# Two cross-attentions on one core: seven of eight context transposes move from TensorE to VectorE, fed by a second, permuted load

## The chip, the cores and the metric

One core of a Trainium2 chip runs the whole program. The metric is device time in microseconds (us). Single instructions are given in ns.

## The reference

```python
# 8 batches; x is 8 x 100 x 128, ctx is 8 x 1444 x 128; 16 heads of width 64
normed = x * rsqrt(mean(x * x) + eps) * norm_w
q, k, v = heads(normed @ wq), heads(ctx @ wk), heads(ctx @ wv)
x = x + (softmax(q @ k.T) @ v) @ wo          # first cross-attention
x = x + softmax(x @ ctx.T) @ ctx             # second one, ctx is key and value
```

## The kernel before

The weights are folded: with Wq·Wk of a head multiplied out beforehand, the keys of all heads are the context itself, and with Wv·Wo multiplied out the values are too. So one batch is 1,600 rows of queries (16 heads x 100), cut into 13 items of up to 124 rows, each against the same 1,444 tokens. The second attention of a batch is one more item of 100 rows ("late" in the code); for batches 0 to 5 it runs in step 8 of the batch after. For precision each operand is split in a high and a low part in fp32r, and three products are summed.

A batch has 14 steps, 0 to 13, written out by hand for each engine. In step s an item is scored, and the item of the step before is turned. "Item 9" below means the item scored in step 9. For it:

- TensorE makes the scores in three chunks of 512, 512 and 420 tokens (`scores`, lines 912, 913, 916), in a ring of four PSUM banks.
- VectorE takes the maximum of each chunk (`chunk_maximum`, L697), and then of the three (L702).
- ScalarE takes the exponentials (`exp_chunk`, L555).
- In the next step TensorE turns the probabilities (`turn`, L940), chunk by chunk, into `ps_t`, which has two banks. A turn waits until the low part of the chunk two turns earlier has been read from its bank (`wait_turn_bank`). The list `TURNS` holds the order.
- ScalarE copies the turned chunk as the high part (`turned_chunk_hi`, L546), and VectorE makes the low part (`turned_chunk_lo`, L683).
- TensorE multiplies turned probabilities with the context (`pv`, L964), 17 matmuls in steps 10 and 11, none in step 12, where the late item's product stands after the turns (`pv_late`, L977 to L981).

The scores need the context with its features on the partitions (`cT_hi`, `cT_lo`). In steps 9, 10 and 11 of batches 0 to 6, TensorE ends its step with four transposes of the next batch's context (`turn_ctx`, L874 and L876; one chunk per step) into the same two banks. ScalarE copies this as `cT_hi` after the second exponential of the step (L612). VectorE makes `cT_lo` (L683) behind the low parts of its step. The order of VectorE in a step is:

```python
chunk_maximum(g, 0)
turned_chunk_lo(prev, 0)
chunk_maximum(g, 1)
chunk_maximum(g, 2)          # and the maximum of the three, L702
turned_chunk_lo(prev, 1)
turned_chunk_lo(prev, 2)
# cT_lo in steps 9, 10, 11; invert; pair_lo
```

Odd batches 1, 3 and 5 make the queries of two later batches in steps 5 to 10, 12 and 13: a pair of heads a step, with a copy on ScalarE (`pair_hi`, L500) ahead of `cT_hi` and one on VectorE (`pair_lo`) behind `cT_lo`. Batch 0 makes the Wv·Wo products in steps 9 to 12 instead (L1033).

The queue of SP loads the context of the next batch in step 2 (`load_ctx`, L322 and three small ones, L324). For each group of items it stores the inverted denominators to DRAM (L361), waits for that, and loads them back broadcast over the partitions (L368). GpSimd multiplies with them (`norm_group`, L437): group 1 in step 7, ahead of its own work on the item of that step (`split_tail`, L429 and L431), which TensorE's third turn of the next step waits for.

Of the kernel before, what the change touches and what calls it, by code (L numbers as in the profile page):

```python
# [16 lines left out]
def bass_two_cross_attentions(nc, x, ctx_in, wq, wk, wv, wo, norm_w, out):  # L17
# [26 lines left out]

    def rows(item):
        return Q if item == LATE else min(TM, R - TM * item)
# [32 lines left out]
    CTX_T_STEPS = [9, 10, 11]  # L79
    CTX_SPLIT = [(0, 4), (4, 8), (8, 12)]  # L80
# [34 lines left out]
    for g, (b, s, _, _) in enumerate(ITEMS):  # L115
        if g > 0 and g < L_FIRST:
            TURNS += [("item", g - 1, c) for c in range(NC)]
        if b < B - 1 and s in CTX_T_STEPS:
            TURNS.append(("ctx", b + 1, CTX_T_STEPS.index(s)))
# [6 lines left out]
    def ev(g, c=NC - 1):  # L126
        return NC * g + c + 1
# [30 lines left out]
    with ExitStack() as stack:  # L158
# [18 lines left out]
        c_both = [sb(f"c_both{i}", [P, SLOTS, 2, D], F32R) for i in range(2)]  # L177
        cT_hi = [sb(f"cT_hi{i}", [P, S], F32R) for i in range(2)]
        cT_lo = [sb(f"cT_lo{i}", [P, S], F32R) for i in range(2)]
        tail_a = sb("tail_a", [P, D])  # L180
# [27 lines left out]
        pT_late = sb("pT_late", [P, SLOTS, 2, Q], F32R)  # L208
# [3 lines left out]
        pT = [sb(f"pT{i}", [P, SLOTS, 2, GW[i]], F32R) for i in range(2)]  # L212
# [73 lines left out]
        ctx_turned = sem("ctx_turned")  # L286
        ctxT_hi = sem("ctxT_hi")
# [31 lines left out]
        def _(sp):  # L319
# [7 lines left out]

            def store_result(b):
                sp.wait_ge(fin_ready, b + 1)
                sp.dma_start(out[b:b + 1, :, :].rearrange("a q d -> (a q) d"), result[0:Q, :])\  # L330
                    .then_inc(stored, 16)
# [13 lines left out]
            for b in range(B):  # L345
                if b < B - 1:
                    sp.wait_ge(ctx_turned, n(b, NC, NC - 1))
                    sp.wait_ge(ctx_lo_done, n(b, len(CTX_SPLIT), len(CTX_SPLIT) - 1))
                    sp.wait_ge(stack_steps, n(b, 3, 2))
                    load_ctx(b + 1)  # L350
                for g in range(NG):
                    if g == NG - 1 and 0 < b < B - 1:
                        store_result(b - 1)
                    if b == B - 1 and g == NG - 1:
                        continue
                    k = NG * b + g
                    t0, count = GROUPS[g][0], len(GROUPS[g])
                    s0 = step_of(t0)
                    cols = slice(TM * t0, TM * (t0 + count))
                    sp.wait_ge(inverted, k + 1)  # L360
                    sp.dma_start(scratch[b:b + 1, cols].rearrange("a (t p) -> p (a t)", p=TM),  # L361
                                 rinv[0:TM, s0:s0 + count],
                                 allow_slow_non_contiguous=True).then_inc(rinv_stored, 16)
                    sp.wait_ge(rinv_stored, 16 * (k + 1))
                    if k >= 2:

                        sp.wait_ge(o_normed, k - 1)
                    sp.dma_start(rinv_row[:, k % 2, 0:TM * count],  # L368
                                 scratch[b:b + 1, cols].to_broadcast([P, TM * count]))\
                        .then_inc(rinv_row_loaded[g], 16)  # L370
# [5 lines left out]
        def _(pool):  # L376
# [9 lines left out]
            pool.memset(ones[:, :], 1.0).then_inc(consts_begun, 1)  # L386
            pool.wait_ge(consts_begun, 6)
# [11 lines left out]
            def split_ctx(b, part):  # L399
                lo, hi = CTX_SPLIT[part]  # L400
                top = min(hi, FULL)
                pool.wait_ge(ctx_hi_done, n(b, len(CTX_SPLIT), part))
                pool.tensor_tensor(c_both[b % 2][:, lo:top, 1, :], ctx_raw[:, lo:top, :],
                                   c_both[b % 2][:, lo:top, 0, :].bitcast(F32),
                                   ALU.subtract).then_inc(ctx_lo_done, 1)

            def stack_tail(b):
# [10 lines left out]
                pool.tensor_tensor(c_both[b % 2][:, FULL, 0, :], tail_a[:, :], tail_b[:, :], ALU.add)\  # L418
# [64 lines left out]
        def _(act):  # L483
# [41 lines left out]
            def ctx_hi(b, part):  # L525
                lo, hi = CTX_SPLIT[part]
                top = min(hi, FULL)
                act.activation(c_both[b % 2][:, lo:top, 0, :], ctx_raw[:, lo:top, :], ACT.Copy)\
                    .then_inc(ctx_hi_done, 1)

            def turned_chunk_hi(g, c):
# [4 lines left out]
                if item == LATE:  # L536
                    if c == 0 and bb > 0:
                        act.wait_ge(pv_done, block(bb - 1, LATE))
                    dst = pT_late[:, j0:j0 + nj, 0, 0:m]
                else:  # L540
                    grp, col = group_of(item), group_col(item)
                    if c == 0 and NG * bb + grp >= 2:
                        b2, g2 = divmod(NG * bb + grp - 2, NG)
                        act.wait_ge(pv_done, block(b2, g2))
                    dst = pT[grp % 2][:, j0:j0 + nj, 0, col:col + m]
# [29 lines left out]
            for b in range(B):  # L575
                for s in range(STEPS):
# [24 lines left out]
                    if here:  # L601
                        for c in range(NC):
# [3 lines left out]
                            if c == 1 and s in CTX_T_STEPS and b < B - 1:  # L606
                                ct = CTX_T_STEPS.index(s)
                                c0, w = CHUNKS[ct]
                                act.wait_ge(ctx_turned, n(b + 1, NC, ct))
                                if ct == 0 and 0 < b < B - 1:  # L610
                                    act.wait_ge(scored, ev(late_number(b - 1)))
                                act.activation(cT_hi[(b + 1) % 2][:, c0:c0 + w],  # L612
                                               ps_t[:, turn_bank("ctx", b + 1, ct), 0:w], ACT.Copy)\
# [40 lines left out]
        def _(dve):  # L654
# [50 lines left out]
            def turned_chunk_lo(g, c):  # L705
# [5 lines left out]
                if item == LATE:  # L711
                    dst, hi = [pT_late[:, j0:j0 + nj, a, 0:m] for a in (1, 0)]
                else:
                    grp, col = group_of(item), group_col(item)
                    dst, hi = [pT[grp % 2][:, j0:j0 + nj, a, col:col + m] for a in (1, 0)]
# [44 lines left out]
            for b in range(B):  # L760
                for s in range(STEPS):
# [15 lines left out]
                    if s in CTX_T_STEPS and b < B - 1:  # L777
# [3 lines left out]
                        lo_part(cT_lo[(b + 1) % 2][:, c0:c0 + w], ps_t[:, turn_bank("ctx", b + 1, ct), 0:w],  # L781
                                cT_hi[(b + 1) % 2][:, c0:c0 + w], ctxT_lo)
                    if prev is not None:
# [44 lines left out]
        def _(pe):  # L828
# [89 lines left out]
            def wait_turn_bank(what, at, c):  # L918
                k = TURNS.index((what, at, c)) - 2
                if k >= 0:  # L920
                    what, at, c = TURNS[k]
                    if what == "ctx":
                        pe.wait_ge(ctxT_lo, n(at, NC, c))
                    else:
                        pe.wait_ge(turned_lo, ev(at, c))
# [18 lines left out]
            def pv(b, grp, lo, hi, by_chunk=False):  # L944
# [13 lines left out]
                for i in range(lo, hi):  # L958
# [3 lines left out]
                    weights = c2[:, j, (0, 0, 1)[part], :]  # L962
                    moving = p[:, j, (0, 1, 0)[part], 0:w]
# [4 lines left out]
            def pv_late(bb, by_chunk=False):  # L968
# [5 lines left out]
                for j in range(FULL):  # L974
                    if by_chunk and j % 4 == 0:
                        pe.wait_ge(turned_lo, ev(g, j // 4))
                    pe.matmul(ps_o[0:Q, 0, 0:2 * D], pT_late[:, j, 0, :],  # L977
                              c2[:, j, :, :].rearrange("p a d -> p (a d)"), start=(j == 0), stop=False)
                    pe.matmul(ps_o[0:Q, 0, 0:D], pT_late[:, j, 1, :], c2[:, j, 0, :],  # L979
                              start=False, stop=False)  # L980
                pe.matmul(ps_o[0:Q, 0, 0:D], pT_late[:, FULL, 0, :], c2[:, FULL, 0, :],  # L981
# [81 lines left out]
            for b in range(B):  # L1063
                for s in range(STEPS):
# [21 lines left out]
                    if s in CTX_T_STEPS and b < B - 1:  # L1086
                        c = CTX_T_STEPS.index(s)
                        if c == 0:
                            pe.wait_ge(ctx_loaded, 64 * (b + 2))
                        wait_turn_bank("ctx", b + 1, c)  # L1090
                        turn_ctx(ps_t[:, turn_bank("ctx", b + 1, c)], c).then_inc(ctx_turned, 1)
# [64 lines left out]
```

## Time and profile before

| | |
|---|---|
| time, median of 3 runs | 699.72 us (698.96 to 700.08) |
| the profiled execution's own time | 699.38 us |
| its span in the profile | 697.6 us |
| TensorE matmul busy | 675.7 us, 97% of the span |
| VectorE busy | 465.6 us, 67% |
| ScalarE busy | 467.8 us, 67% |
| GpSimd busy | 160.7 us, 23% |
| mean granted clock of TensorE | 0.995 |
| DMA packets | 25,566 |

PE is the matmul side of TensorE, DVE is VectorE, ACT is ScalarE, POOL is GpSimd, SPq is the queue of SP. A busy share says how much of the span an engine had an instruction under way. It does not say how late the next one can come.

### The profile page before, as it was taken

The page shows a single profiled execution, that of the slowest core. Times are in us where ns is not written, and L with a number is a line of the kernel's source. Part 1 is how long each engine was busy: PE and PEld are TensorE (multiplying, and loading weights), DVE is VectorE, ACT ScalarE, POOL GpSimd, SP SyncE. Part 2 cuts the span into 40 slices and gives each one's busy share as a digit, 9 for nine tenths or more (in the row PEclk, how much of TensorE's full clock was granted, in tenths as well). Part 3 has the DMA queues.
Part 4 walks back from the last instruction along what each step waited for, and adds up shares of the span by engine and source line. Part 5 has one row for each costly group of instructions (what it writes and reads, how often), then busy time and mean ns, then how long its engine had stood idle before and what let it go on. Part 6 is the DMA issues. An engine that isn't in the chain of part 4 may idle for free. (4 is left out here: it accounts for less than half of the span.)

```text
span 697.6 us, 13322 instructions
## 1 busy us (share of the span) xinstructions
PE 675.7 (97%) x4764; PEld 613.6 (88%) x4764; DVE 465.6 (67%) x994; ACT 467.8 (67%) x1169; POOL 160.7 (23%) x485
## 2 busy tenths in 40 slices
PE   5899999999999999999999999999999999999986
PEld 4688989998999889999899889999899888999885
DVE  3586666777567875677666775677766776577733
ACT  4767676677666766667766776667766777666742
POOL 2211133111322114111142114211142212422110
PEclk9999999999999999999999999999999999999997
DMA  6012112111021002220121111202013011112000
GB/s 188 1 54 16 8 12 53 16 8 9 15 55 15 16 1 23 53 16 8 16 51 11 16 9 15 55 14 16 1 15 60 9 16 15 9 9 16 9 12 7
DMA packets 25566, 16.50 MB, mean 24 GB/s; under 512 B 14334, under 2 KB 23838, under 8 KB 25502
## 3 DMA queue, kind: packets, MB, share of 16 engines
q1 hardware_dynamic: 25502, 15.66, 14.7%
q8 instruction: 39, 0.64, 0.5%
q14 instruction: 25, 0.20, 0.2%
HBM read 15.19 MB, written 0.46 MB: 22 GB/s over the span
## 5 line engine op out<-in xcount | busy, mean ns | idle before, releaser
L546 ACT ACTIVATE pT<-ps_t 128x496 fp32r<-128x496 f32 (+1 forms) x312 | 182.4, 587 | 179.8 <-PE ps_t L940 177.6
L697 DVE TENSOR_REDUCE part_max<-ps_s 124x1 f32<-124x512 f32 (+2 forms) x336 | 209.5, 651 | 60.1 <-PE ps_s L916 59.0
L964 PE MATMUL ps_o<-pT,c_both 128*128 128x248 f32 (+2 forms) x1632 | 242.9, 291 | 0.6 <-DVE result L748 0.5
L683 DVE TENSOR_TENSOR pT<-ps_t,pT 128x496 fp32r<-128x496 f32 (+3 forms) x312 | 192.0, 623 | 69.5 <-ACT pT L546 67.7
L964 PEld LDWEIGHTS ps_o<-pT,c_both 128*128 128x128 f32 x1632 | 219.4, 189 | 3.6 <-DVE pT L683 2.6
L555 ACT ACTIVATE probs<-ps_s,neg_max 124x512 f32<-124x512 f32 (+2 forms) x336 | 219.1, 663 | 1.4 <-DVE neg_max L702 1.4
L940 PE MATMUL ps_t<-ident,probs 124*128 124x124 f32 (+2 forms) x1232 | 184.1, 268 | 5.1 <-DVE pT L683 1.9
L940 PEld LDWEIGHTS ps_t<-ident,probs 124*128 124x128 f32 (+2 forms) x1232 | 146.1, 140 | 44.8 <-ACT probs L555 10.1
L429 POOL CAST tails<-probs 124x36 fp32r<-124x36 f32 (+2 forms) x224 | 40.6, 213 | 489.7 <-ACT probs L555 489.7
L912 PE MATMUL ps_s<-cT_hi,q_hi 128*124 128x512 f32 (+3 forms) x312 | 143.5, 460 | 1.2 <-DVE q_lo L683 1.2
L916 PE MATMUL ps_s<-cT_hi,q_lo 128*124 128x512 f32 (+3 forms) x312 | 118.8, 381 | 0.0
L913 PE MATMUL ps_s<-cT_lo,q_hi 128*124 128x512 f32 (+3 forms) x312 | 118.6, 380 | 0.0
L555 ACT ACTIVATION_READ_ACCUMULATOR probs<-ps_s,neg_max 124x1 f32 (+2 forms) x336 | 70.2, 209 | 0.0
L916 PEld LDWEIGHTS ps_s<-cT_hi,q_lo 128*124 128x124 f32 (+1 forms) x312 | 57.2, 183 | 10.8
L912 PEld LDWEIGHTS ps_s<-cT_hi,q_hi 128*124 128x124 f32 (+1 forms) x312 | 57.9, 186 | 2.1 <-issue 0.8
L913 PEld LDWEIGHTS ps_s<-cT_lo,q_hi 128*124 128x124 f32 (+1 forms) x312 | 58.3, 187 | 0.1
L683 DVE TENSOR_TENSOR cT_lo<-ps_t,cT_hi 128x512 fp32r<-128x512 f32 (+1 forms) x23 | 15.2, 662 | 34.3 <-ACT cT_hi L612 29.2
L683 DVE TENSOR_TENSOR q_lo<-ps_m,q_hi 128x400 fp32r<-128x400 f32 x31 | 17.7, 572 | 30.5 <-ACT q_hi L500 30.5
L437 POOL TENSOR_TENSOR o_norm<-o_norm,rinv_row 128x248 f32<-128x248 f32 (+2 forms) x47 | 35.8, 761 | 3.4 <-ACT o_norm L562 3.3
L986 PE MATMUL ps_m<-o_norm,wvo 128*128 128x100 f32 x256 | 33.0, 272 | 1.6 <-DVE o_norm L740 1.6
L986 PEld LDWEIGHTS ps_m<-o_norm,wvo 128*128 128x128 f32 x256 | 31.4, 191 | 1.8 <-DVE o_norm L740 1.8
L431 POOL TENSOR_TENSOR tails<-probs,tails 124x36 fp32r<-124x36 f32 (+2 forms) x112 | 29.3, 261 | 9.0
(130 smaller groups left out, 492.8 us busy)
## 6 DMA issues: line engine op xcount, KB each, us to landing
ctx_raw<-in_ctx_dram SPq DMA_DIRECT2D x8, 704.0 KB
rinv_row<-denominator_rows SPq DMA_DIRECT2D x39, 124.0 KB, 3.7
rinv_row<-denominator_rows SPq DMA_DIRECT2D x8, 186.0 KB, 3.5
denominator_rows<-rinv SPq DMA_DIRECT2D x39, 1.0 KB
wq_sb<-in_L_xattn_wq_dram SPq DMA_DIRECT2D x2, 256.0 KB, 6.1
wk_sb<-in_L_xattn_wk_dram SPq DMA_DIRECT2D x2, 256.0 KB, 6.3
wv_sb<-in_L_xattn_wv_dram SPq DMA_DIRECT2D x1, 512.0 KB, 7.8
wo_sb<-in_L_xattn_wo_dram SPq DMA_DIRECT2D x1, 512.0 KB, 8.9
```

What stands on the lines that cost most here:

```text
L429: pool.tensor_copy(t[0:m, c * TAIL:(c + 1) * TAIL].bitcast(F32R), src).then_inc(tail_hi, 1)
L437: pool.tensor_tensor(o_norm[:, group_cols(g)], o_norm[:, group_cols(g)], rinv_row[:, (NG * b + g) % 2, 0:group_width(g)], ALU.mult).then_i ...
L546: act.activation(dst, ps_t[:, turn_bank("item", g, c), 0:nj * m] .rearrange("p (j m) -> p j m", m=m), ACT.Copy).then_inc(turned_hi, 1)
L555: act.activation(probs[g % 2][0:m, c0:c0 + w], ps_s[0:m, score_bank(g, c), 0:w], ACT.Exp, bias=neg_max[0:m, k:k + 1], accum_out=sums[0:m, ...
L683: dve.tensor_tensor(dst, src, hi.bitcast(F32), ALU.subtract).then_inc(done, 1)
L697: mx = dve.tensor_reduce(part_max[0:m, k, c:c + 1], ps_s[0:m, score_bank(g, c), 0:CHUNKS[c][1]], AX.X, ALU.max)
L912: pe.matmul(dst, a_hi, cT_hi[bb % 2][:, c0:c0 + w], start=True, stop=False)
L913: pe.matmul(dst, a_hi, cT_lo[bb % 2][:, c0:c0 + w], start=False, stop=False)
L916: pe.matmul(dst, a_lo, cT_hi[bb % 2][:, c0:c0 + w], start=False, stop=True).then_inc(scored, 1)
L940: t = pe.transpose(ps_t[:, turn_bank("item", g, c), m * (j - j0):m * (j - j0 + 1)], src, ident[0:m, 0:m])
L964: t = pe.matmul(ps_o[:, 0, 0:w], weights, moving, start=(i == 0), stop=(i == UNITS - 1))
L986: t = pe.matmul(ps_m[:, 0, 0:Q], wvo[:, head_cols(h)], o_norm[:, Q * h:Q * (h + 1)], start=(h == 0), stop=(h == H - 1))
```

## The change

In batches 1 to 7 the context is not transposed by TensorE any more. SP loads each of them a second time, permuted, into `ctx_q`: partition 32i + a holds features 32i to 32i + 31 of token (r, a), so a transpose of each block of 32 x 32 gives the turned context. The load is 24 DMAs in pieces of 32 features, which is 128 bytes. It stands in SP's order ahead of the store of group 1. VectorE does the block transposes (512, 512 and 448 columns) at the end of steps 7, 8 and 10 into `cT_raw`, a staging tile for two chunks. `cT_hi` and `cT_lo` are made from there in steps 9, 10 and 11, as before. The turns of the context leave the list `TURNS`. `c_both`, `pT` and `pT_late` lose one unused row each (indices `his` and `los`), and their strides stay the same. Batch 0 keeps its transposes on TensorE.

```diff
-        if b < B - 1 and s in CTX_T_STEPS:
-            TURNS.append(("ctx", b + 1, CTX_T_STEPS.index(s)))
...
-        c_both = [sb(f"c_both{i}", [P, SLOTS, 2, D], F32R) for i in range(2)]
+        c_both = [sb(f"c_both{i}", [P, 2 * FULL + 1, D], F32R) for i in range(2)]
...
+        ctx_q = sb("ctx_q", [P, NR, 32])
+        cT_raw = sb("cT_raw", [P, 2, 512])
...
+            def load_ctx_q(b):
+                blocks, rest = (S - FULL * P) // 32, TAIL % 32
+                for i in range(4):
+                    part, col = slice(32 * i, 32 * (i + 1)), slice(32 * i, 32 * (i + 1))
+                    for r4 in range(4):
+                        at = 32 * FULL * r4
+                        sp.dma_start(ctx_q[part, r4:4 * FULL:4, :],
+                                     ctx_in[b, at:at + 32 * FULL, col].rearrange("(a j) c -> a j c", j=FULL))\
+                            .then_inc(ctx_q_loaded, 16)
+                    sp.dma_start(ctx_q[part, 4 * FULL:4 * FULL + blocks, :],
+                                 ctx_in[b, FULL * P:FULL * P + 32 * blocks, col]
+                                 .rearrange("(r a) c -> a r c", a=32)).then_inc(ctx_q_loaded, 16)
+                    sp.dma_start(ctx_q[32 * i:32 * i + rest, 4 * FULL + blocks, :],
+                                 ctx_in[b, S - rest:S, col]).then_inc(ctx_q_loaded, 16)
...
-                    sp.wait_ge(ctx_turned, n(b, NC, NC - 1))
+                    if b == 0:
+                        sp.wait_ge(ctx_turned, NC)
+                        sp.wait_ge(ctx_q_cleared, 1)
...
                 for g in range(NG):
+                    if g == 1 and b < B - 1:
+                        if b > 0:
+                            sp.wait_ge(ctx_flipped, NC * b)
+                        load_ctx_q(b + 1)
...
+            pool.memset(ctx_q[:, NR - 1, :], 0.0).then_inc(ctx_q_cleared, 1)
...
-                                act.wait_ge(ctx_turned, n(b + 1, NC, ct))
+                                act.wait_ge(ctx_flipped, NC * b + ct + 1)
...
-                                act.activation(cT_hi[(b + 1) % 2][:, c0:c0 + w],
-                                               ps_t[:, turn_bank("ctx", b + 1, ct), 0:w], ACT.Copy)\
+                                act.activation(cT_hi[(b + 1) % 2][:, c0:c0 + w], cT_raw[:, ct % 2, 0:w], ACT.Copy)\
...
-                        lo_part(cT_lo[(b + 1) % 2][:, c0:c0 + w], ps_t[:, turn_bank("ctx", b + 1, ct), 0:w],
+                        lo_part(cT_lo[(b + 1) % 2][:, c0:c0 + w], cT_raw[:, ct % 2, 0:w],
                                 cT_hi[(b + 1) % 2][:, c0:c0 + w], ctxT_lo)
+                    if s in FLIP_STEPS and b < B - 1:      # FLIP_STEPS = [7, 8, 10]
+                        ct = FLIP_STEPS.index(s)
+                        r0, r1 = CHUNKS[ct][0] // 32, -(-(CHUNKS[ct][0] + CHUNKS[ct][1]) // 32)
+                        dve.wait_ge(ctx_q_loaded, 16 * 24 * (b + 1))
+                        if b > 0 or ct == NC - 1:
+                            dve.wait_ge(ctxT_lo, n(b + 1, NC, 0) if ct == NC - 1 else n(b, NC, ct))
+                        dve.transpose(cT_raw[:, ct % 2, 0:32 * (r1 - r0)],
+                                      ctx_q[:, r0:r1, :].rearrange("p r c -> p (r c)")).then_inc(ctx_flipped, 1)
...
-                    if s in CTX_T_STEPS and b < B - 1:
-                        c = CTX_T_STEPS.index(s)
-                        if c == 0:
-                            pe.wait_ge(ctx_loaded, 64 * (b + 2))
-                        wait_turn_bank("ctx", b + 1, c)
-                        turn_ctx(ps_t[:, turn_bank("ctx", b + 1, c)], c).then_inc(ctx_turned, 1)
```

## Rows read from the trace of the kernel before

**Rows 1.** The page, its first part: busy time, share of the span, instructions.
```profile
PE 675.7 (97%) x4764; PEld 613.6 (88%) x4764; DVE 465.6 (67%) x994; ACT 467.8 (67%) x1169; POOL 160.7 (23%) x485
```

**Rows 2.** Timeline of PE, batch 3, steps 9 to 12: start, us, what, idle before.
```profile
320.41 0.60 PE L874 MATMUL ps_t<-ident,ctx_raw 128*128 128x128 f32 x4
320.77 0.48 PE L912 MATMUL ps_s<-cT_hi,q_hi 128*124 128x512 f32 x1
...
332.54 0.55 PE L874 MATMUL ps_t<-ident,ctx_raw 128*128 128x128 f32 x3
...
333.20 0.50 PE L912 MATMUL ps_s<-cT_hi,q_hi 128*124 128x512 f32 x1
...
336.21 0.51 PE L940 MATMUL ps_t<-ident,probs 124*128 124x124 f32 x3
```

**Rows 3.** Timeline of DVE, batch 3, steps 9 to 12.
```profile
321.98 0.69 DVE L683 TENSOR_TENSOR cT_lo<-ps_t,cT_hi 128x512 fp32r<-128x512 f32 x1 [1.58 <-ACT cT_hi L612]
...
325.71 0.15 DVE L702 TENSOR_REDUCE neg_max<-part_max 124x1 f32<-124x3 f32 x1
...
328.26 0.69 DVE L683 TENSOR_TENSOR cT_lo<-ps_t,cT_hi 128x512 fp32r<-128x512 f32 x1 [1.36 <-ACT cT_hi L612]
...
331.75 0.16 DVE L702 TENSOR_REDUCE neg_max<-part_max 124x1 f32<-124x3 f32 x1
...
335.39 0.68 DVE L683 TENSOR_TENSOR pT<-ps_t,pT 128x496 fp32r<-128x496 f32 x1
```

**Rows 4.** Timeline of ACT, batch 3, steps 9 to 11.
```profile
321.33 0.61 ACT L612 ACTIVATE cT_hi<-ps_t 128x512 fp32r<-128x512 f32 x1
...
325.90 0.69 ACT L555 ACTIVATE probs<-ps_s,neg_max 124x512 f32<-124x512 f32 x1
...
332.17 0.68 ACT L555 ACTIVATE probs<-ps_s,neg_max 124x512 f32<-124x512 f32 x1
```

**Rows 5.** Groups of instructions by form: busy us, mean ns, idle before.
```profile
L697 DVE TENSOR_REDUCE part_max<-ps_s 124x1 f32<-124x512 f32 x192 | 131.2, 683 | 52.6 <-PE ps_s L916 52.6
```

**Rows 6.** Timeline of DVE, batch 2, steps 10 and 11.
```profile
242.99 0.16 DVE L702 TENSOR_REDUCE neg_max<-part_max 124x1 f32<-124x3 f32 x1
...
248.59 0.16 DVE L702 TENSOR_REDUCE neg_max<-part_max 124x1 f32<-124x3 f32 x1
```

**Rows 7.** Timeline of ACT, batch 2, steps 10 and 11.
```profile
243.62 0.68 ACT L555 ACTIVATE probs<-ps_s,neg_max 124x512 f32<-124x512 f32 x1
...
249.47 0.68 ACT L555 ACTIVATE probs<-ps_s,neg_max 124x512 f32<-124x512 f32 x1
```

**Rows 8.** Timeline of PE, batch 0, step 12.
```profile
91.17 0.51 PE L940 MATMUL ps_t<-ident,probs 124*128 124x124 f32 x3 [0.22 <-DVE pT L683]
```

**Rows 9.** Timeline of ACT, batch 0, step 11.
```profile
87.98 0.52 ACT L612 ACTIVATE cT_hi<-ps_t 128x420 fp32r<-128x420 f32 x1 [0.84 <-PE ps_t L876]
```

**Rows 10.** Timeline of SP's queue, batch 2, steps 2 to 5.
```profile
199.46 1.20 SPq L324 DMA_DIRECT2D ctx_raw<-in_ctx_dram  x3
...
207.57 0.35 SPq L368 DMA_DIRECT2D rinv_row<-denominator_rows  x1
214.19 0.26 SPq L361 DMA_DIRECT2D denominator_rows<-rinv  x1
220.20 0.34 SPq L368 DMA_DIRECT2D rinv_row<-denominator_rows  x1
```

**Rows 11.** DMA issues of the page: count, KB each, median us to landing.
```profile
rinv_row<-denominator_rows SPq DMA_DIRECT2D x39, 124.0 KB, 3.7
```

**Rows 12.** Timeline of POOL, batch 2, steps 7 and 8.
```profile
226.48 0.73 POOL L437 TENSOR_TENSOR o_norm<-o_norm,rinv_row 128x248 f32<-128x248 f32 x1
230.78 0.36 POOL L429 CAST tails<-probs 124x36 fp32r<-124x36 f32 x2 [3.57 <-ACT probs L555]
```

**Rows 13.** DMA view, 11 to 13 us: packets, MB, share of 16 engines.
```profile
q1 hardware_dynamic: 931, 0.62, 104.7%
```

**Rows 14.** DMA view, 304.8 to 310.2 us: one store of inverted denominators.
```profile
q1 hardware_dynamic: 252, 0.00, 2.6%
```

## The prediction on record

> **What bounds the kernel now.** I read the page first: TensorE's matmul side is busy for 97% of the span [rows 1]. So an instruction taken from it gives time back, as long as the next one is not then waiting for somebody else. The second view was therefore the timeline of the three engines over steps 9 to 12, where the transposes stand. I read it for a batch of each kind: odd with query pairs (1, 3, 5), even without (2, 4, 6), and batch 0. The others of a kind repeat it to within 0.1 us.
>
> In batch 3, look at how late VectorE is. It makes `cT_lo` at 321.98 and at 328.26, each time right after `cT_hi` [rows 3, 4]. From 328.26 it has no idle time until the maximum of the three at 331.75: `cT_lo`, the pair's low part, a maximum, a low part and two maxima, 3.49 us. The exponential of item 10 starts 0.19 us after the start of its maximum (325.71 to 325.90). That of item 11 starts at 332.17, only 0.23 us later than its own maximum would allow (331.75 + 0.19 = 331.94). Then the third turn of item 11 starts at 336.21, 0.14 us after the end of the low part that frees its bank (335.39 + 0.68 = 336.07) [rows 2, 3]. In step 12 no `pv` stands ahead of this turn, so it has no cover. TensorE looks busy there, but this place is set by the chain ScalarE, VectorE, bank.
>
> **What is removed.** In each of seven batches, 12 transposes leave TensorE. Its next scores start 0.36 us after the first group of four (320.41 to 320.77) and 0.66 us after the third (332.54 to 333.20) [rows 2]. The second is like the first. That is 0.36 + 0.36 + 0.66 = 1.38 us a batch, and 9.7 us over seven. This is the most that the freed work alone can give. With waits for the two banks, of which the 0.22 us in batch 0 is one [rows 8], I put it at about 12 us at most.
>
> **What is added to VectorE.** A block transpose is not in this trace. The nearest row is a VectorE instruction that reads 512 fp32 columns, 683 ns long [rows 5]; such ones follow each other every 0.59 us. Below that nothing speaks for a price: 448 columns at the same pace are 0.53 us. From above, if a 4-byte element took two passes, it would be double, 1.1 us. I take 0.53 us for the 448 columns of step 10 and 0.59 us for the other two, the pace of all VectorE instructions of this length here. The copies of `cT_raw` have the lengths of those they replace, and I cost the new source at nothing in either direction.
>
> The Trainium skill (VectorE: DVE Perf Modes, The three transpose paths) gives 311 ns for a bf16 128 x 128 on VectorE against 390 ns on TensorE. By that the engines cost about the same for one transpose, and the move would be a plain gain; no run here shows either number.
>
> The transposes of steps 7 and 8 fall into idle time of VectorE: after them it waits for ScalarE for 0.3 us or more beyond what they take. I cost them at nothing. If they were 1.1 us long, step 8 would lose some 0.3 us. The third, in step 10, stands behind `cT_lo` of step 10, just in the stretch without idle time.
>
> **Odd batches.** Nothing that the change removes comes ahead of the chain. It begins at `cT_hi` at 321.33, which follows two exponentials and a pair's high part on ScalarE, all fed by turns before step 9 ends. So the maximum of item 10 at 325.71, its exponential at 325.90 and `cT_lo` at 328.26 stay where they are, though TensorE arrives earlier. Then the block transpose is put in: the maximum of item 11 goes to 331.75 + 0.53 = 332.28, its exponential to 332.47, which is 0.30 us later than 332.17. From there to the third turn of item 11 each link is an instruction of ScalarE or VectorE right behind another (336.21 - 332.17 = 4.04 us), so this turn is 0.30 us late as well. TensorE has been relieved of 1.38 us by then, and waits all of it off. Three odd batches: +0.9 us.
>
> **Even batches.** The exponential of item 10 starts at 243.62, but its maximum allows 242.99 + 0.19 = 243.18 [rows 6, 7]. The turn that held it back comes earlier now, so it gains 0.44 us. That of item 11 has 249.47 - (248.59 + 0.19) = 0.69 us of such slack. Its maximum moves by -0.44 + 0.53 = +0.09 us, so the exponential moves by 0.09 - 0.69 = -0.60 us. The same chain then leads to the third turn. Three even batches: -1.8 us.
>
> **Batch 0.** Here ScalarE waits for the transposes themselves, 0.84 us in step 11 [rows 9], since the Wv·Wo products stand ahead of them. With the data there beforehand, the chain moves forward, and the full price comes back, with the bank wait: 1.38 + 0.22 = 1.60 us.
>
> **The load.** In batch 2 the 24 DMAs start behind 207.57 at 0.40 us each (1.20 for three), 9.6 us, until 217.6 [rows 10]. The store of group 1 stands behind them, at 217.6 instead of 214.19. The load after it comes 6.0 us after the store (214.19 to 220.20), at 223.6, and lands 3.7 us later [rows 11], at 227.3. `norm_group` of group 1 on GpSimd was at 226.48 and moves by 0.8 us. Behind it is queued the tail of item 7, at 230.78 [rows 12]; with 0.73 us for the norm, the landing has until 230.0. So 2.7 us are left, and I cost the move at nothing. `ctx_q` itself is needed only at the end of step 7, 229.5. The load of `ctx_raw` waits for the same things as before in batches 1 to 6.
>
> This holds if the 16 DMA engines keep pace: 5,776 packets of 128 bytes, 364 for each with rounding. The nearest rows are 252 packets, nearly all of 4 bytes: 0.026 x 16 x 5.4 us / 252 = 9 ns each [rows 14]; and 931 of 666 bytes in the mean: 1.047 x 16 x 2 us / 931 = 36 ns [rows 13]. At 9 ns the load is bound by its issue. At 36 ns it ends at 208.7 + 364 x 0.036 = 221.8, a backlog of some 3 us behind the last issue, which just fits. I take about 20 ns, between the two and nearer the small one in size.
>
> **Sum.** -1.6 - 1.8 + 0.9 = -2.5 us. It is made against the profiled execution, 699.38 us (its span, 697.6, and 1.8 around it). That lies 0.34 below the median of the runs, so 699.72 - 2.5 gives 697.2 us.
>
> **Rivals.** (1) The transposes' time comes back in full: -9.7 us, with bank waits -12, so 687.5 to 690. For it speaks 97% busy, against it that the low part at 335.39 already ends just ahead of the turn that it frees, with a longer queue now. It needs a chain shorter by over a microsecond. Chance 0.07.
>
> (2) The load falls behind: the price of a packet decides, from about 39 ns on (222.8 - 208.7 over 364, where the limit is the landing at 230.0 to 230.8). Then GpSimd waits in step 7 for `rinv_row`, the tail of item 7 is late, and TensorE stands in step 8. At 45 ns it is 2.2 us a batch, at double the 36 ns 12 us a batch: +15 to +84 us, 715 to 784. Against it is that smaller packets cost less in the two rows. Chance 0.13.
>
> The Trainium skill (DMA: Bandwidth & Descriptors, the table at its head) says that transfers under 512 B make the DMA engine read, modify and write. By that rule rival 2 is the result, near its upper end; the stores of 4 bytes at 9 ns here do not show such a price, but they go to DRAM.
>
> (3) The block transpose takes two passes, 1.1 us. The odd batches lose 0.9 us each, the even ones nothing, batch 0 keeps its 1.6: 2.7 - 1.6 + 0.3 for step 8 = +1.4 us, 701.1. Rows of this trace neither show nor exclude it. Chance 0.13.
>
> The forecast has 0.67.
>
> **How the numbers follow.** A measurement of this kernel can tell about 0.2% from no change, 1.4 us: faster is below 698.3, slower above 701.1. The forecast's own range is 695.5 to 699.5: 0.3 us a batch for links that I read as fixed. Of its 0.67 some 0.53 are faster, 0.14 the same. Rival 1 is all faster, rival 2 all slower, rival 3 half the same and half slower. That gives faster 0.60, same 0.21, slower 0.19. For 8 in 10, the range runs from 693.5, which leaves out most of rival 1, to 701.5, which takes in rival 3 and leaves out rival 2.
>
> **What would show it.** Right: in odd batches the third turn of item 11 follows its low part by 0.14 us, and TensorE idles about 1.7 us in steps 10 to 12; the maximum of item 11 stands about 4.0 us behind `cT_lo` instead of 3.49; batch 0 is shorter by 1.6 us. GpSimd's norm of group 1 waits less than 1 us. Wrong: a stall of TensorE on `tails` in step 8, a block transpose far from 0.6 us, a wait of VectorE for `ctx_q` in step 7, or a total gain near 10 us, which would mean that the chain is not what sets step 12.

## The result, and the profile after

The changed kernel takes 704.71 us (median of four runs, 702.53 to 706.84). The kernel before took 699.85 us beside it (four runs, 698.96 to 700.08). The ratio is 1.0073, 95% interval 1.0052 to 1.0095: slower by 0.7%, where 0.36% faster was forecast, and outside the range. The profiled execution is the fastest of the four: 702.53 us, span 700.8. So the trace has 3.2 us of the 4.9 to explain.

The page of the kernel after, its first part and the hardware queue's line:

```profile
PE 666.5 (95%) x4680; PEld 604.8 (86%) x4680; DVE 477.5 (68%) x1015; ACT 467.0 (67%) x1169; POOL 160.6 (23%) x486
...
q1 hardware_dynamic: 68286, 20.84, 20.5%
```

TensorE gave up 9.2 us of work [rows 1], and the span grew by 3.2. So 12.4 us of idle time were added. The view of waits of the kernel after (us in total, times, longest) names a wait on a DMA that the same view of the kernel before does not have:

```profile
POOL o_norm L473 <- DMA rinv_row<-denominator_rows: 37.5, 7, 6.4
...
PEld ps_t L981 <- POOL tails L467: 5.6, 5, 1.9
...
PE ps_t L981 <- POOL tails L467: 4.3, 4, 1.6
```

It is followed from its cause. SP's queue in batch 2, to be held against [rows 10]:

```profile
206.22 0.35 SPq L403 DMA_DIRECT2D rinv_row<-denominator_rows  x1
206.62 2.98 SPq L348 DMA_DIRECT2D ctx_q<-in_ctx_dram  x4
209.64 0.61 SPq L351 DMA_DIRECT2D ctx_q<-in_ctx_dram  x1
210.29 0.32 SPq L354 DMA_DIRECT2D ctx_q<-in_ctx_dram  x1
...
218.16 2.54 SPq L348 DMA_DIRECT2D ctx_q<-in_ctx_dram  x4
220.75 0.60 SPq L351 DMA_DIRECT2D ctx_q<-in_ctx_dram  x1
221.39 0.32 SPq L354 DMA_DIRECT2D ctx_q<-in_ctx_dram  x1
221.76 0.30 SPq L396 DMA_DIRECT2D denominator_rows<-rinv  x1
227.34 0.35 SPq L403 DMA_DIRECT2D rinv_row<-denominator_rows  x1
```

The 24 DMAs hold the queue from 206.62 to 221.76, 15.1 us. In these 15.1 us the 16 DMA engines are busy for 41% of their time, so they have time to spare. Next, look at who needs the row of group 1. POOL and PE of the kernel after, steps 7 and 8 of batch 2:

```profile
231.31 0.71 POOL L473 TENSOR_TENSOR o_norm<-o_norm,rinv_row 128x248 f32<-128x248 f32 x1 [6.43 <-DMA rinv_row<-denominator_rows]
231.96 0.36 POOL L465 CAST tails<-probs 124x36 fp32r<-124x36 f32 x2
232.41 0.26 POOL L467 TENSOR_TENSOR tails<-probs,tails 124x36 fp32r<-124x36 f32 x1
```

```profile
230.62 0.48 PE L981 MATMUL ps_t<-ident,probs 124*128 124x124 f32 x3
232.72 0.33 PE L981 MATMUL ps_t<-ident,tails 124*128 124x124 f32 x1 [1.62 <-POOL tails L467]
```

The norm stood at 226.48 [rows 12] and now waits 6.43 us for the row. The tails of item 7 are queued behind it, and TensorE stands for them. By the starts of its steps (first score matmul to the first of the next step), that step 8 is 0, 1.86, 0.60, 1.37, 0.31 and 1.40 us longer in batches 1 to 6: 5.5 us.

Steps 9 to 12, read in the same way, against the kernel before (us):

| batches | step 9 | step 10 | step 11 | step 12 | sum | forecast |
|---|---|---|---|---|---|---|
| 0 | -0.41 | -0.40 | -0.64 | -0.27 | -1.72 | -1.60 |
| 1, 3, 5 | -0.51 | +0.03 | +0.12 | +0.76 | +0.40 each | +0.30 each |
| 2, 4, 6 | -0.83 | 0.00 | -0.36 | +0.68 | -0.51 each | -0.60 each |

That makes -2.0 us, and with the 5.5 of step 8 and a start that is 0.3 earlier the 3.2 of the span. The chain looks as it was forecast. DVE in batch 3 of the kernel after, to be held against [rows 3]:

```profile
328.66 0.69 DVE L718 TENSOR_TENSOR cT_lo<-cT_raw,cT_hi 128x512 fp32r<-128x512 f32 x1 [1.39 <-ACT cT_hi L648]
329.27 0.64 DVE L825 STREAM_TRANSPOSE cT_raw<-ctx_q 128x448 f32<-128x448 f32 x1
329.83 0.53 DVE L718 TENSOR_TENSOR q_lo<-ps_m,q_hi 128x400 fp32r<-128x400 f32 x1
...
332.68 0.16 DVE L737 TENSOR_REDUCE neg_max<-part_max 124x1 f32<-124x3 f32 x1
...
336.13 0.68 DVE L718 TENSOR_TENSOR pT<-ps_t,pT 128x496 fp32r<-128x496 f32 x1
```

and PE there, to be held against the last row of [rows 2]:

```profile
331.69 0.51 PE L981 MATMUL ps_t<-ident,probs 124*128 124x124 f32 x3 [0.55 <-DVE pT L718]
...
336.95 0.51 PE L981 MATMUL ps_t<-ident,probs 124*128 124x124 f32 x3 [0.79 <-DVE pT L718]
```

The maximum of item 11 is 4.02 us behind `cT_lo` (332.68 - 328.66), and the third turn starts 0.14 us after its low part ends (336.13 + 0.68 = 336.81). With 0.46 us in step 10, TensorE idles 1.80 us in this batch's steps 10 to 12, where about 1.7 was forecast.

### The profile page after: what moved, and what is told of

Its sections match the earlier page's. It is cut to its first block and busy times, and to the rows that moved or that the text cites. A ratio compares the mean times of both kernels' runs of the same rounds, so it can differ in the third digit from the quotient of the medians.

```text
span 700.8 us, 13357 instructions
## 1 busy us (share of the span) xinstructions
PE 666.5 (95%) x4680; PEld 604.8 (86%) x4680; DVE 477.5 (68%) x1015; ACT 467.0 (67%) x1169; POOL 160.6 (23%) x486
## 2 busy tenths in 40 slices
DMA packets 68351, 21.69 MB, mean 31 GB/s; under 512 B 57118, under 2 KB 66622, under 8 KB 68286
## 3 DMA queue, kind: packets, MB, share of 16 engines
q1 hardware_dynamic: 68286, 20.84, 20.5%
## 5 line engine op out<-in xcount | busy, mean ns | idle before, releaser
L582 ACT ACTIVATE pT<-ps_t 128x496 fp32r<-128x496 f32 (+1 forms) x312 | 180.5, 587 | 186.3 <-PE ps_t L981 184.6
L981 PE MATMUL ps_t<-ident,tails 124*128 124x124 f32 (+2 forms) x112 | 30.1, 269 | 4.4 <-POOL tails L467 4.3
```

The source lines that it names most:

```text
L582: act.activation(dst, ps_t[:, turn_bank("item", g, c), 0:nj * m] .rearrange("p (j m) -> p j m", m=m), ACT.Copy).then_inc(turned_hi, 1)
L981: t = pe.transpose(ps_t[:, turn_bank("item", g, c), m * (j - j0):m * (j - j0 + 1)], src, ident[0:m, 0:m])
```

## The experiments

The theory after the result (T): the chain in steps 9 to 12 is worth -2 us, and the load of `ctx_q` costs it all by its place and length in SP's queue. The rivals: the stall is caused by the 128-byte packets in the DMA engines, or the loss comes from VectorE's new reads and transposes.

### The load taken away (e1), and the load alone (e2)

`e1_load_once` fills `ctx_q` once, for batch 1, and transposes it again in every batch. It leaves out the loads for batches 2 to 7, whose turned context is then that of batch 1:

```
-                    if g == 1 and b < B - 1:
-                        if b > 0:
-                            sp.wait_ge(ctx_flipped, NC * b)
+                    if g == 1 and b == 0:
                         load_ctx_q(b + 1)
...
-                        dve.wait_ge(ctx_q_loaded, 16 * 24 * (b + 1))
+                        dve.wait_ge(ctx_q_loaded, 16 * 24)
```

> The permuted load is made once, for batch 1, and left out for batches 2 to 7, whose turned contexts are then those of batch 1; all else is the changed kernel. Theory A (the 24 DMAs take 15 us of SP's queue, so the denominators of group 1 come late and TensorE stands in step 8; the chain of steps 9 to 12 by itself gains 2 us): the 5.5 us of step 8 go, the rest stays: 2.0 us below the kernel before, 697.8 us. Rival B (the block transposes on VectorE are what costs, the load is free): stays near the changed kernel, 703 to 705 us.

Measured: 697.62 us (8 runs, 696.25 to 698.67), ratio 0.9973 (0.9962 to 0.9984). Step 8 has its old length, and steps 9 to 12 are those of the changed kernel to within 0.03 us. So these two parts are independent, and VectorE's part is a gain.

`e2_load_only` keeps the load and puts the transposes back on TensorE; `cT_hi` and `cT_lo` are made from `ps_t` again, and the loaded `ctx_q` is not used:

```
+        if b < B - 1 and s in CTX_T_STEPS:
+            TURNS.append(("ctx", b + 1, CTX_T_STEPS.index(s)))
...
-                    if s in FLIP_STEPS and b < B - 1:
+                    if False:
```

> The permuted load stays in its place, but nobody uses it: TensorE transposes the contexts as in the kernel before, VectorE makes no block transposes. Theory A: steps 8 of batches 2 to 6 stall as in the changed kernel, +5 to +6 us against the kernel before, 705 us, and nothing changes in steps 9 to 12. Rival B: same time as the kernel before, 699.9 us.

Measured: 706.05 us (6 runs, 701.74 to 709.98), ratio 1.0078 (1.0050 to 1.0107). The load alone makes the kernel slower. Its profiled execution is the slowest of its runs. Step 8 is longer by 0.38, 1.63, 2.10 and 2.21 us in batches 1, 2, 4 and 6. Steps 9 and 10 together are longer as well in batches 4 and 6, by 1.4 us in each of the two, where nothing was expected. The row of PE in front of step 9 of batch 6, and then a row of its scores:

```profile
568.03 0.33 PE L988 MATMUL ps_t<-ident,tails 124*128 124x124 f32 x1 [2.00 <-POOL tails L470]
...
569.18 0.63 PE L961 MATMUL ps_s<-cT_lo,q_hi 128*124 128x512 f32 x1
```

Such a matmul takes 0.40 us elsewhere. The view of stretches of the same kernel, where the column after the busy times is the granted clock:

```profile
566.00:568.00 2.00, 0.03 (x1) 0.00 (x0) 1.04 (x3) 0.00 (x0) 1.27 (x4) 1.00 0.11 10
568.90:571.50 2.60, 2.60 (x11) 2.04 (x10) 1.49 (x5) 2.51 (x8) 0.45 (x3) 0.52 0.00 0
```

TensorE stood for 2.00 us, and soon after it was granted 0.52 of its speed, the 1.2 GHz level, for some microseconds. A stall can thus cost more than its own length. It does not always: in `e6_four_big`, described below, the clock stays at 1.00 behind a stall of 3.52 us that ends at 155.37, and falls to 0.50 behind one of 3.54 us that ends at 505.16:

```profile
155.40:158.40 3.00, 3.00 (x20) 2.74 (x21) 1.70 (x5) 2.67 (x7) 0.00 (x0) 1.00 0.02 5
...
505.20:508.40 3.20, 3.20 (x12) 3.17 (x13) 1.37 (x4) 2.04 (x6) 0.00 (x0) 0.50 0.23 2
```

So the length of a stall alone does not tell whether the clock falls.

### The load moved (e3), and the norm moved (e10)

`e3_spread` leaves every instruction of the other engines as in the changed kernel and only cuts the load into quarters, each behind a `rinv_row` load whose successor has time:

```
-                    if g == 1 and b < B - 1:
-                        if b > 0:
-                            sp.wait_ge(ctx_flipped, NC * b)
-                        load_ctx_q(b + 1)
...
+                    if g == 0 and b < B - 1:
+                        load_ctx_q(b + 1, (2,) if b > 0 else (0, 1, 2))
+                    elif g == 1 and b < B - 1:
+                        load_ctx_q(b + 1, (3,))
+                    elif g >= 4 and b < B - 2:
+                        sp.wait_ge(ctx_flipped, NC * (b + 1))
+                        load_ctx_q(b + 2, (g - 4,))
```

> The same 24 DMAs, but in four quarters of six, each behind the load of a group's denominators (groups 4 and 5 of the batch before, 0 and 1 of this one). Theory A: no row of denominators is late by more than a microsecond, no stall in step 8, so the same as the load made once, 697.8 us. Rival C (it is the traffic of 42,800 small packets, wherever it stands, that slows other transfers): a stall of the same size somewhere else, 703 us or more.

Measured: 697.74 us (11 runs, 695.96 to 698.39), ratio 0.9975 (0.9966 to 0.9983). SP's queue of `e3_spread` in batch 2:

```profile
207.82 0.35 SPq L399 DMA_DIRECT2D rinv_row<-denominator_rows  x1
208.22 2.54 SPq L348 DMA_DIRECT2D ctx_q<-in_ctx_dram  x4
210.80 0.61 SPq L351 DMA_DIRECT2D ctx_q<-in_ctx_dram  x1
211.45 0.32 SPq L354 DMA_DIRECT2D ctx_q<-in_ctx_dram  x1
213.34 0.27 SPq L392 DMA_DIRECT2D denominator_rows<-rinv  x1
```

A DMA of the load takes the queue as long as before, but the store waits for nobody. The same bytes in the same packets then cost nothing: e3 stands where e1 does.

`e10_norm_later` is the opposite test. The load stays whole and in place, and the norm of group 1 goes from step 7 to step 9 on GpSimd, off the tails' queue:

```
-                    if s in EVAC and b + EVAC[s][1] >= 0:
+                    if s in EVAC and s != 7 and b + EVAC[s][1] >= 0:
                         norm_group(b + EVAC[s][1], EVAC[s][0])
+                    if s == 9:
+                        norm_group(b, 1)
```

> The changed kernel with its load where it was, but GpSimd normalizes group 1 in step 9 instead of step 7, ahead of its work on item 9. Theory A (the only harm of the late row is that the tail of item 7 is queued behind the norm of group 1 on GpSimd): no stall in step 8, 697.8 us, though the row lands as late as before. Rival C (the load harms something else as well, such as its own use in step 7 or the transfers of later groups): 700 us or more.

Measured: 698.01 us (11 runs, 697.12 to 698.66), ratio 0.9984 (0.9975 to 0.9993). Step 8 has its old length in all batches. The late row does harm only because the tails are queued behind the norm.

### Fewer, larger DMAs (e6)

A piece is one row of 32 features, 128 bytes. Of the 24 DMAs of a load, 16 have 352 pieces, four have 32 and four have 4. If SP pays for each DMA, four DMAs over all 128 partitions in place of sixteen over 32 shorten the load. If it pays for each piece, they don't.

```
+                for r4 in range(4):
+                    at = 32 * FULL * r4
+                    sp.dma_start(ctx_q[:, r4:4 * FULL:4, :],
+                                 ctx_in[b, at:at + 32 * FULL, :].rearrange("(a j) (i c) -> i a j c", j=FULL, i=4))\
+                        .then_inc(ctx_q_loaded, 16)
```

> The permuted load in its place of the changed kernel, but the 16 DMAs of 32 partitions are 4 DMAs of 128 partitions and 1408 pieces each; same packets, same bytes. Theory A1 (SP pays about 0.64 us for each DMA, whatever it holds): 12 DMAs take 6 us, the store of group 1 is hardly late, no stall in step 8: 697.8 us. Rival A2 (SP pays for each piece): 4 times 2.5 us, the store stays 7 us late, and the time stays near the changed kernel, 703 to 706 us.

Measured: 736.20 us (5 runs, 735.79 to 739.45), ratio 1.0543 (1.0522 to 1.0563), far beyond both expectations. SP's queue of `e6_four_big` in batch 2:

```profile
213.59 12.46 SPq L346 DMA_DIRECT2D ctx_q<-in_ctx_dram  x4
226.09 3.33 SPq L351 DMA_DIRECT2D ctx_q<-in_ctx_dram  x1
...
232.20 0.30 SPq L396 DMA_DIRECT2D denominator_rows<-rinv  x1
237.90 0.35 SPq L403 DMA_DIRECT2D rinv_row<-denominator_rows  x1
```

The load is 18.6 us long (213.59 to 232.20), where the two theories expected 6 and 10 us. The first row merges four DMAs of 1408 pieces. Taken alone, the first of them, and then a DMA of 32 pieces further on, behind one of 4 pieces:

```profile
213.59 0.59 SPq L346 DMA_DIRECT2D ctx_q<-in_ctx_dram  x1
...
229.82 0.32 SPq L351 DMA_DIRECT2D ctx_q<-in_ctx_dram  x1
```

The first one holds the queue no longer than one of 352 pieces does in `e3_spread` (0.57 us, at 208.22). The next three take 4.40, 3.50 and 3.85 us, and the DMA of 32 pieces right behind them takes 3.33, where one of the same size takes 0.32 further on. In the changed kernel a DMA of 32 pieces takes 0.60 us right behind one of 352. So a DMA is held long where a large one stands right ahead of it, and its own pieces alone do not give its time. Why a large one holds the next for so long stays open. This run also walks the pieces of a DMA in another order, and from 220 to 226 us the DMA engines are busy for 33% of their time, where those of the changed kernel are for 48% from 208 to 215. So it does not separate the two prices.

Step 8 is 2.9 to 5.9 us longer in batches 1 to 6, 28.6 us in all. The stall in batch 2 is 4.95 us; from 243 to 246, around its end, TensorE is granted 0.50 of its speed, and step 9 is 1.0 us longer than before the change, where that of the changed kernel is 0.8 us shorter.

### The transpose on VectorE (e5, e4)

`e5_spread_double` is e3 with the transpose of step 10 done twice in a row:

```
+                        if ct == NC - 1:
+                            dve.transpose(cT_raw[:, 0, 0:32 * (r1 - r0)],
+                                          ctx_q[:, r0:r1, :].rearrange("p r c -> p (r c)")).then_inc(ctx_flip_extra, 1)
+                            dve.wait_ge(ctx_flip_extra, b + 1)
```

> The spread load, with the third block transpose of step 10 made twice over. Theory D (the chain of ScalarE and VectorE sets steps 10 to 12 of batches 1 to 6): one more link of 0.55 us in each of six batches, nothing in batch 0, +3.3 us against the spread one's 697.7, 701.0 us. Rival E (VectorE has 32% idle time and hides it): 697.7 us.

Measured: 701.12 us (5 runs, 700.13 to 702.65), ratio 1.0034 (1.0021 to 1.0046). It is 3.4 us above e3, whose runs were made on another chip. Step 11 is 0.66 us longer in each of batches 1 to 6 and as long as before in batch 0. DVE of `e5_spread_double`, batch 3:

```profile
328.26 0.64 DVE L830 STREAM_TRANSPOSE cT_raw<-ctx_q 128x448 f32<-128x448 f32 x1
328.93 0.65 DVE L833 STREAM_TRANSPOSE cT_raw<-ctx_q 128x448 f32<-128x448 f32 x1
```

So a transpose at this place has its full price in six batches, and the chain has no slack to take it up. The 0.66 us is the price of one that the next has to wait for: the second starts 0.67 us after the first here, while `q_lo` follows the single one of the changed kernel after 0.56 (329.27 to 329.83).

`e4_spread_flip_first` puts the block of the transpose ahead of the `cT_lo` block in VectorE's program:

```
+                    if s in FLIP_STEPS and b < B - 1:
+                        ...
                     if s in CTX_T_STEPS and b < B - 1:
                         ...
-                    if s in FLIP_STEPS and b < B - 1:
```

> As the spread load, and the third block transpose, in step 10, stands ahead of cT_lo of that step, where VectorE waits 1.3 us for ScalarE, instead of behind it. Theory D (steps 9 to 12 are set by the chain of ScalarE and VectorE, and the third transpose lengthens it by 0.55 us in six batches): 0.55 x 6 = 3.3 us below the spread one, 694.5 us; the maximum of item 11 follows cT_lo of step 10 by 3.5 us again in odd batches. Rival E (the order within VectorE's step does not matter, the engine only has more to do): same as the spread one, 697.8 us.

Measured: 694.49 us (5 runs, 692.82 to 695.73), ratio 0.9927 (0.9914 to 0.9939). DVE of `e4_spread_flip_first`, batch 3:

```profile
323.14 0.64 DVE L822 STREAM_TRANSPOSE cT_raw<-ctx_q 128x448 f32<-128x448 f32 x1
324.62 0.69 DVE L721 TENSOR_TENSOR cT_lo<-cT_raw,cT_hi 128x512 fp32r<-128x512 f32 x1 [0.84 <-ACT cT_hi L651]
...
328.11 0.16 DVE L740 TENSOR_REDUCE neg_max<-part_max 124x1 f32<-124x3 f32 x1
```

The transpose runs while VectorE waits for `cT_hi`, 0.84 us of that wait are left, and the maximum is 3.49 us behind `cT_lo` again, as it was before the change. Each of six batches gives back 0.53 us in step 11.

### What sets the rest (e7, e8, e9)

`e7_spread_lag` takes VectorE's wait for `cT_hi` away: `cT_lo` of a chunk is made one step later, in steps 10, 11 and 12, when `cT_hi` is long there.

```
+    CTX_LO_STEPS = [10, 11, 12]
...
-                    if s in CTX_T_STEPS and b < B - 1:
-                        ct = CTX_T_STEPS.index(s)
+                    if s in CTX_LO_STEPS and b < B - 1:
+                        ct = CTX_LO_STEPS.index(s)
```

> The spread load, and cT_lo one step later than cT_hi (steps 10, 11, 12 for 9, 10, 11), so that VectorE does not wait 1.1 to 1.6 us for ScalarE at the end of each step; the same instructions. Theory D: the chain loses its longest wait, and TensorE gets most of the freed 1.4 to 2.0 us a batch in batches 1 to 6: 689 to 692 us. Rival E: order does not matter, 697.7 us.

Measured: 690.93 us (4 runs, 689.51 to 692.61), ratio 0.9885 (0.9869 to 0.9901). Steps 10 and 11 now give back time, but step 12 is still 0.7 us longer than before the change. `e8_spread_lag_hi_last` also makes `cT_hi` last on ScalarE in its step:

```
-                            if c == 1 and s in CTX_T_STEPS and b < B - 1:
+                            if c == NC - 1 and s in CTX_T_STEPS and b < B - 1:
```

> As the lagged one, and ScalarE makes cT_hi behind the third exponential of the step instead of the second. Theory D: the third exponential comes 0.6 us earlier, but it is not the one that TensorE waits for, so at most 1 us more, 689 to 691 us. Rival: the high parts of the turned chunks behind it are unchanged, so no difference at all from the lagged one.

Measured: 691.82 us (4 runs, 690.07 to 692.45), ratio 0.9893 (0.9879 to 0.9907). It tells nothing from e7: the place of `cT_hi` on ScalarE is then no part of what binds.

`e9_lag_late_split` is e7 with cover for step 12. The matmuls of the late product that were all behind the third turn are split, four pairs of them ahead of it:

```
+                    late_here = s == LATE_PV_STEP and 0 < b < B - 1
+                    if late_here:
+                        pv_late(b - 1, hi=4)
...
-                    if s == LATE_PV_STEP and 0 < b < B - 1:
-                        pv_late(b - 1)
+                    if late_here:
+                        pv_late(b - 1, lo=4)
```

> As the lagged one, and in step 12 of batches 1 to 6 the first 8 of the 23 matmuls of the late item stand ahead of the third turn of item 11 instead of behind it; no instruction is added or taken. Theory D (this turn waits about 0.7 us for the low part that frees its bank, because no work stands ahead of it in step 12): 0.65 us x 6 = 3.9 us below the lagged one's 690.9, 687.0 us. Rival E (TensorE is the bound and the order does not matter): 690.9 us.

Measured: 686.52 us (4 runs, 685.53 to 686.65), ratio 0.9815 (0.9802 to 0.9829): the best version, 1.85% faster than the kernel before. PE of `e7_spread_lag` at the third turn of item 11 in batch 3:

```profile
330.58 0.35 PE L964 MATMUL ps_s<-cT_hi,q_lo 128*124 128x420 f32 x1
331.69 0.51 PE L985 MATMUL ps_t<-ident,probs 124*128 124x124 f32 x3 [0.76 <-DVE pT L722]
```

and of `e9_lag_late_split`:

```profile
328.77 0.32 PE L1023 MATMUL ps_o<-c_both,pT_late 128*100 128x256 f32 x1
328.93 0.22 PE L1025 MATMUL ps_o<-c_both,pT_late 128*100 128x128 f32 x1
329.08 0.51 PE L985 MATMUL ps_t<-ident,probs 124*128 124x124 f32 x3
```

The late matmuls fill the 0.76 us, and step 12 goes from +0.7 to -0.12 us (odd) and -0.20 (even) against the kernel before.

## Why the prediction was wrong

**The step that failed: the load, costed at nothing.** It took "0.40 us each (1.20 for three)" for the 24 DMAs [rows 10]. Those rows are of DMAs with 36 pieces. Here 16 of the 24 have 352 pieces and take 0.65 us from one to the next (2.54 for four). The four of 32 pieces right behind them take 0.65 as well, the four of 4 pieces 0.36, and with two longer ones it is 15.1 us in place of 9.6. The store is 5.5 us later than it was put, the next load comes 5.6 us after it (6.0 taken), and the row lands 4.0 us later (3.7 taken). The spare 2.7 us are overdrawn by 2.8. In batch 2 the tails are 2.8 us late on the run's own time (231.96, where 230.78 less the 1.64 us by which this step starts earlier is 229.14), and TensorE, which had about 1 us of its own before it needs them, is 1.86 us late. The 5.5 us in all turned -2.0 into +3.5. That the load, standing whole ahead of the store in SP's queue, is the cause is shown by e1, e2 and e3, and that it works through the norm in GpSimd's order is shown by e10.

The Trainium skill (DMA: Bandwidth & Descriptors, Anatomy of one DMA) puts down descriptor generation as small, and says that many can be emitted before a cost shows; that account is for DMAs issued by GpSimd. On SP here each DMA of 352 pieces of 128 bytes takes the queue for 0.65 us in a row of such ones.

**Rival 2 had the place, but not the mechanism.** Its stall on the tails in step 8 came, though the engines kept pace. Per packet the load cost 0.205 x 16 x 700.8 - 0.147 x 16 x 697.6 = 658 us over 68,286 - 25,502 = 42,784 packets, where 0.147 and 25,502 are those of the page before: 15 ns, below the 20 that were taken and far from the 39 that would decide. From 215 to 221.7 us of the changed kernel, where the load runs almost alone, it is 0.327 x 16 x 6.7 us / 2,795 = 12.5 ns. So this rival, weighed at 0.13 by a packet's price, lacked the issue price, the time that a DMA takes of SP's queue, which decided at some 0.5 us for each DMA (2.7 us of spare over 24, beside 0.40). The trace of the kernel before could warn of such a price, but not give it. Its SP queue at the start:

```profile
0.79 0.39 SPq L333 DMA_DIRECT2D x_rows<-in_x_dram  x1
...
6.05 0.71 SPq L343 DMA_DIRECT2D wo_sb<-in_L_xattn_wo_dram  x1
```

The first has 800 pieces of 512 bytes and nothing ahead of it, the last has 1,024 pieces and stands behind other large loads. Counting pieces would not have been enough: 128 pieces take 0.34 to 0.36 us in the loads of `rinv_row` and `ctx_raw`.

The Trainium skill (DMA: Bandwidth & Descriptors, the table at its head) says that transfers under 512 B are read, modified and written. That does not show here as a higher price of a packet: 15 ns for 128 bytes, with 36 ns for 666 [rows 13].

**The chain was right.** -1.72 us in batch 0 for -1.60, +0.40 for +0.30, -0.51 for -0.60: together -2.0 for -2.5. The transpose was priced right: in batch 3 it puts 4.02 - 3.49 = 0.53 us between `cT_lo` and the maximum, as taken. What was mis-sized is `cT_hi`, whose new source was costed at nothing. ScalarE in batch 3 of the kernel before, step 10:

```profile
327.63 0.60 ACT L612 ACTIVATE cT_hi<-ps_t 128x512 fp32r<-128x512 f32 x1
328.11 0.63 ACT L555 ACTIVATE probs<-ps_s,neg_max 124x420 f32<-124x420 f32 x1
```

and of the kernel after:

```profile
328.00 0.64 ACT L648 ACTIVATE cT_hi<-cT_raw 128x512 fp32r<-128x512 f32 x1
328.51 0.62 ACT L591 ACTIVATE probs<-ps_s,neg_max 124x420 f32<-124x420 f32 x1
```

What stands behind the copy starts 0.03 us later (0.51 for 0.48). With the copies of steps 9 and 11 (0.04 and 0.05 us) this accounts for the 0.1 us by which each odd batch is worse than forecast; the even ones miss by the same 0.1. e4 shows that the chain carries the transpose one for one, e7 that the wait for `cT_hi` in it was worth more (6.8 us from e3 to e7) than all that the change gave back (2.0), and e9 that the rest stood in step 12 without cover.

**Rival 1** (all of it back) is false for the change as made, and e9 shows what it lacked: with the load out of the way, `cT_lo` a step later and the late product split, 12.8 us are gained (699.33 to 686.52). Part of this comes from waits that the kernel before had as well, so it is not the value of the transposes alone; no run makes these two moves in the kernel before. **Rival 3** (two passes, 1.1 us) is false by the durations, 0.64 and 0.70 us.

**What stays open.** The timed runs reach 706.84, 4.3 us above the profiled one, while those of e1, e3 and e10, which have no stall, lie within 2.5 us of each other. The clock behind a stall of e2 (0.52) would make such a scatter. In e2 the slower runs have the lower mean granted clock: 0.995 for 701.74 us, 0.991 and 0.992 for 707.97 and 708.17, 0.986 for 709.98. In the changed kernel it explains a part at most: 0.995 for the profiled 702.53 us, 0.993 for 704.87 and 706.84, but 0.995 again for 704.56. Its trace has 1.00 behind its stall of 1.62 us, and its slower runs have no trace. So the cause of the last 1.7 us of the loss is not shown. It is also open why a large DMA holds the queue for the next one as long as it does.

## What to carry to other kernels

Cost a DMA in the queue that issues it by a row of the same shape with the same large DMAs ahead of it, not by the nearest DMA's duration. Where there is no such row, leave a wide range. Then follow what is queued behind it to the consumer that stands in front of another's work. Work moved off the busiest engine gives back time only after the chain that it joins has been shortened: here the transposes gave 2 us, and the places of two further blocks 11 more.

## What the runs showed of the hardware

- SP's queue is held longer where a DMA stands right behind a large one. Behind one of 352 pieces the next took 0.60 to 0.62 us, though it had only 32 pieces; behind one of 1408 (e6) it took 3.33 us with 32 pieces. Behind one of 4 pieces, 32 pieces took 0.32 us (e6). The first large one of a group took 0.57 us with 352 pieces (e3) and 0.59 with 1408 (e6), and DMAs of 128 pieces took 0.34 to 0.36.
- After TensorE idled 1.88 and 2.00 us (e2) or 4.95 us (e6), its granted clock was at the 1.2 GHz level (0.50 to 0.52) for the next few microseconds, and a score matmul of 0.40 us took 0.63. After 1.42 us (e2) and 1.62 us (the changed kernel) it was 1.00. But it was 1.00 after 3.52 us in e6 too, and near the end of the kernel before it was 0.50 from 680 to 683 us, after an idle time of only 1.65 us that ended at 678.34. So the length of one idle time does not decide it alone.
- A store of the denominators that is issued right behind a broadcast load takes longer. In the changed kernel the next load follows such a store after 7.1 to 8.6 us (14 places, the store at most 1.4 us behind the load), and after 5.1 to 6.8 us in the 33 others. For example, it is 7.4 us for the store of 227.74, and 5.6 for that of 221.76, which stands behind the load of `ctx_q`.
